# A quarter of the state sum of a scan kernel moved from VectorE to ScalarE and TensorE, with one decay bank fewer

## The reference, cut to what matters

```python
dt = softplus(xc @ dt_w + dt_b);  A = -exp(A_log)
Bm = xc @ B_w;  Cm = xc @ C_w
def step(h, inp):                       # once per token, h is [batch, 512, 16]
    h = exp(dt_t[..., None] * A) * h + dt_t[..., None] * Bm_t * xc_t[..., None]
    y = einsum('bds,bs->bd', h, Cm_t) + D_skip * xc_t
out = ys @ out_proj_w
```

## Time and profile before

| | us |
|---|---|
| median of 3 executions | 1931.46 (1931.4 to 1935.31) |
| the profiled execution | 1939.45 |
| its span in the trace | 1937.8 |
| phase 1, scans of the eight chunks | 80 to 1134.6 of the span |
| a chunk between two starts of scans | 133.5 to 136.4 (the first 118.0, the last 127.6) |
| phase 2 | from about 1200 |
| VectorE busy in the span | 1256.9 |
| GpSimd, ScalarE | 1016.0, 778.9 |
| TensorE, products | 1524.1 |

### The profile page before, as it was taken

One profiled execution on the slowest core, in us unless ns is written; L12 is line 12 of the kernel. 1 busy time (PEld: TensorE's weight loads), 2 busy tenths in 40 slices (PEclk: granted clock), 3 DMA queues, 4 the chain that ended last, 5 costly groups with the idle time before them and its releaser, 6 DMA issues. The chain is left out here.

```text
span 1937.8 us, 22792 instructions
## 1 busy us (share of the span) xinstructions
PE 1524.1 (79%) x6572; PEld 996.6 (51%) x6572; DVE 1256.9 (65%) x2109; ACT 778.9 (40%) x1378; POOL 1016.0 (52%) x1238
## 2 busy tenths in 40 slices
PE   5787888888887888878876665699999999999600
PEld 2344545545544445445445443467777777777400
DVE  1399999999999999998999962112222222222266
ACT  3555456466465566474563432112211222212122
POOL 0669678788688698687787744011111111111274
PEclk9898899999999999999997597799999999999855
DMA  3111121121122012111111101661101111111165
GB/s 90 50 33 47 42 55 47 58 60 52 53 56 71 27 61 76 39 55 60 46 48 60 49 33 62 222 229 34 33 31 33 32 33 33 33 33 33 41 194 174
DMA packets 78326, 122.22 MB, mean 63 GB/s; under 512 B 12256, under 2 KB 47936, under 8 KB 78208
## 3 DMA queue, kind: packets, MB, share of 16 engines
q1 hardware_dynamic: 60640, 80.12, 13.5%
q0 software_dynamic: 13344, 36.46, 5.9%
q10 hardware_dynamic: 4224, 4.19, 0.6%
HBM read 89.15 MB, written 31.59 MB: 62 GB/s over the span
## 5 line engine op out<-in xcount | busy, mean ns | idle before, releaser
L856 POOL TENSOR_TENSOR bb<-u,br 128x512 f32<-128x512 f32 x512 | 647.6, 1273 | 204.5 <-DVE hh L707 202.9
L591 ACT ACTIVATE bA<-dt,a_neg 128x512 f32<-128x512 f32 x512 | 351.5, 690 | 448.3 <-DVE hh L707 447.6
L466 PE MATMUL bH<-ident,hh 128*128 128x128 f32 x2048 | 344.1, 296 | 166.6 <-DVE hh L707 116.5
L466 PEld LDWEIGHTS bH<-ident,hh 128*128 128x128 f32 x2048 | 259.5, 151 | 412.3 <-DVE hh L707 180.0
L724 DVE SCALAR_TENSOR_TENSOR yT<-bH,bc,yT 128x512 f32<-128x512 f32 x480 | 348.4, 726 | 17.6 <-PE bH L466 17.0
L707 DVE TENSOR_TENSOR_SCAN hh<-bA,hl,bb 128x512 f32<-128x512 f32 x256 | 325.4, 1271 | 1.1 <-ACT bA L591 1.1
L707 DVE TENSOR_TENSOR_SCAN hh<-bA,bb 128x512 f32<-128x512 f32 x256 | 309.2, 1209 | 25.0 <-ACT bA L591 15.9
L1249 POOL DMA_DIRECT2D expert_out_scratch<-yt x71 | 38.7, 544 | 481.7 <-DVE yt L1331 472.5
L1120 PE MATMUL bD<-w_d,hT 128*128 x852 | 197.6, 382 | 0.8 <-ACT hT L1291 0.8
L1285 ACT ACTIVATE sgm<-bG 128x352 f32<-128x352 f32 x142 | 58.1, 461 | 325.6 <-PE bG L1077 325.6
L1077 PE MATMUL bG<-w_g,xtT 128*128 x568 | 181.9, 463 | 1.9 <-DMA w_d<-in_L_ffn_Wd_dram 1.3
(11 more groups left out here) (185 smaller groups left out, 1861.2 us busy)
## 6 DMA issues: line engine op xcount, KB each, us to landing
br<-b_scratch SPq DMA_DIRECT2D x128, 256.0 KB, 3.2
xt<-expert_in_scratch POOLq DMA_DIRECT2D x71, 128.0 KB, 2.3
expert_out_scratch<-yt POOLq DMA_DIRECT2D x71, 128.0 KB, 2.0
w_g<-in_L_ffn_Wg_dram SPq DMA_DIRECT2D x8, 704.0 KB, 4.3
w_u<-in_L_ffn_Wu_dram SPq DMA_DIRECT2D x8, 704.0 KB, 5.9
w_d<-in_L_ffn_Wd_dram SPq DMA_DIRECT2D x8, 640.0 KB, 7.0
xp<-in_L_attn_x_dram SPq DMA_DIRECT2D x8, 512.0 KB, 5.0
xr<-in_L_attn_x_dram SPq DMA_DIRECT2D x8, 512.0 KB, 5.0
```

Source lines behind the costliest of these rows:

```text
L466: i = e.transpose(bH[g % NH][:, q * P:(q + 1) * P], hh[:, (n - 1) % 2, q, d * P:(d + 1) * P], ident[:])
L591: e.activation(bA[g % NA][:], dt[c % 2][:, d, :], ACT.Exp, scale=a_neg[:, d, n:n + 1]).then_inc(s_a, 1)
L856: e.tensor_tensor(bb[:, k % NB, :], u[c % 2][:, d, :], br[:, n % NR, :], ALU.mult).then_inc(s_bb, 1)
```

## The change

Row tile d = 0 of each state leaves VectorE. ScalarE multiplies the transposed tile by its column of C into `hs` (two buffers; `act_sum`), and TensorE adds `hs` by a product with the identity into a bank of its own, `bY`, over the 16 states (`pe_add`, in the slot of d = 2). After the last state ScalarE copies `bY` to `yT` (`act_summed`, slot 3 of the next loop). The bank comes from the decays: `NA` is 2, and with it `AHEAD_ACT` is 1. `summed` replaces the waits on a sum, by the semaphore of the engine that does it.

```diff
-NA, NH, NQ = 3, 2, 3
+NA, NH, NQ = 2, 2, 3
...
+        hs = sb("hs", [P, 2, CH])
...
+        bY = bank("bY")
...
+        def summed(e, m):
+            if m % J:
+                e.wait_ge(s_y, (J - 1) * (m // J) + m % J)
+            else:
+                e.wait_ge(s_hs, m // J + 1)
...
             if g >= ND + NH:
-                e.wait_ge(s_y, g - ND - NH + 1)
+                summed(e, g - ND - NH)
...
+        def pe_add(e, c, k):
+            n, d = divmod(k, ND)
+            q = c * NS + n - 1
+            if d != 2 or q < 0:
+                return
+            e.wait_ge(s_hs, q + 1)
+            if q % NS == 0 and q:
+                e.wait_ge(s_y0, q // NS)
+            e.matmul(bY[:], ident[:], hs[:, q % 2, :], start=(q % NS == 0), stop=(q % NS == NS - 1)).then_inc(s_ya, 1)
...
+        def act_sum(e, c, k):
+            n, d = divmod(k, ND)
+            q = c * NS + n - 1
+            if d or q < 0:
+                return
+            e.wait_ge(s_ht, J * q + 1)
+            if q >= 2:
+                e.wait_ge(s_ya, q - 1)
+            if n == 1:
+                emptied(e, "bc", c)
+            cs = q // NS
+            e.activation(hs[:, q % 2, :], bH[(c * SLOTS + k) % NH][:], ACT.Identity, scale=bc[cs % 2][:, 0, NS + q % NS:NS + q % NS + 1]).then_inc(s_hs, 1)
+
+        def act_summed(e, c, k):
+            if k == 3 and c:
+                e.wait_ge(s_ya, NS * c)
+                e.copy(yT[(c - 1) % 2][:, 0, :], bY[:]).then_inc(s_y0, 1)
...
-            if g < ND:
+            if g < ND or d == 0:
                 return
...
                     if 0 <= loop < NCH:
                         act_main(e, loop, k)
+                    if 0 <= loop < NCH or loop == NCH and k < ND:
+                        act_sum(e, loop, k)
+                        act_summed(e, loop, k)
...
                         pe_main(e, loop, k)
+                        pe_add(e, loop, k)
```

More of the change, by code:

```diff
@@ L215, in phase1 @@
         s_cx = sem("s_cx"); s_nx = sem("s_nx"); s_co = sem("s_co"); s_no = sem("s_no"); s_cl = sem("s_cl"); s_nl = sem("s_nl")
-        s_cr = sem("s_cr"); s_cp = sem("s_cp"); s_te = sem("s_te"); s_on = sem("s_on"); s_rt = sem("s_rt")
+        s_cr = sem("s_cr"); s_cp = sem("s_cp"); s_te = sem("s_te"); s_on = sem("s_on"); s_rt = sem("s_rt"); s_hs = sem("s_hs"); s_ya = sem("s_ya"); s_y0 = sem("s_y0")
         s_m = sem("s_m"); s_e2 = sem("s_e2"); s_pos = sem("s_pos"); s_sc = sem("s_sc"); s_shs = sem("s_shs")
@@ L381, in pe_post @@
                 if k == POST[b]:
-                    e.wait_ge(s_y, SLOTS * (c + 1))
+                    e.wait_ge(s_y, (J - 1) * NS * (c + 1))
+                    e.wait_ge(s_y0, c + 1)
                     room(e, b, c)
@@ L513, in act_proj @@
                 if c >= 2:
-                    e.wait_ge(s_y, SLOTS * (c - 1))
+                    e.wait_ge(s_y, (J - 1) * NS * (c - 1))
                 e.copy(bc[par][:].rearrange("p j s -> p (j s)"), at("bc", c)[:, 0:J * 2 * NS]).then_inc(freesem("bc", c), 1)
@@ L718, in dve_sum @@
             if n == 1:
-                if d == 0:
+                if d == 1:
                     emptied(e, "bc", c)
@@ L722, in dve_sum @@
             else:
-                e.wait_ge(s_y, g - 2 * ND + 1)
+                summed(e, g - 2 * ND)
                 e.scalar_tensor_tensor(out=yy[:, d, :], in0=bH[g % NH][:], scalar=cm, in1=yy[:, d, :],
```

## The result

Over six executions each, the changed kernel takes 1914.69 us (1908.72 to 1921.6) and the kernel before 1933.54 (1931.4 to 1936.81): ratio 0.9896, 95% interval 0.9875 to 0.9916, so about 20 us less (18.9 between the medians). The forecast was 24.6 us less and 1907; the time lies in its range, and the direction is the forecast's.

The account below looks back on a forecast made before the run. VectorE, almost without a gap, was taken to bound the eight state space chunks. 82.6 us removed less 7.9, 11.2, 16.8, 7.7, 6.0 and 8.4 of losses left 24.6 us: median 1907, range 1882 to 1936.

Parts of the forecast that it names:

- What it removes: One of four sums on VectorE, 128 in all, each counting its 0.645 us step: 82.6 us off, the ceiling.
- The scaled copy on ScalarE: 128 scaled copies taken at 0.65 us a step, lying under VectorE's scan in an ordinary slot.
- The silu block at slot 13: ScalarE's table loads and silu make slot 15's decay late: 17.2 us over seven chunks, 11.2 net of what returns.
- Slot 32: Four normalisations behind the new sum stall slot 34 by 0.35 us, the late copy adds 0.8: 7.7 us lost.
- Slot 45: The same normalisation block makes slot 47's decay late, 1.0 us in each of six chunks: 6.0 us lost.
- Slots 56 to 63: ScalarE's block at slots 58, 59 makes slot 61's decay late: 2.4 us on average, chunks 1 to 7, 16.8.
- GpSimd: Even chunks' slots 0 and 4 gain nothing, slots 43 to 57 lose 1.0 us, chunk 0 1.5: 8.4 us.
- TensorE: 128 new products, 110 us of work, mostly hidden; excess at slots 0 to 6, 16 to 19, 24 to 31: 7.9 us.
- Rival 1: ScalarE's stalls idle TensorE and its clock drops, 1.3 us more a block: 34 us, 1941, slower; chance 0.17.
- Rival 2: TensorE bounds slots 0 to 20, costing 24 us more: 1931, about no change; chance 0.08.
- Rival 3: Larger gain: only the two silu blocks count, 46.6 us gained, 1885; chance 0.10.
- the real price: With two decay banks, each decay serves a scan one slot earlier, so ScalarE's blocks at slots 13, 32, 45, 58-59 stall VectorE.

Follow-up runs that it names:

- e1: Kernel before with two decay banks in place of three and nothing else; 1945.94 us, ratio 1.0092 to the kernel before.
- e3: Changed kernel without the identity product on TensorE, with two decay banks; 1912.78 us, ratio 0.9924 to the kernel before.
- e5: Changed kernel with ScalarE's four normalisations of slot 32 moved to slot 33; 1904.65 us, ratio 0.987 to the kernel before.
- e2: Changed kernel without the identity product on TensorE, with three decay banks; 1894.5 us, ratio 0.9832 to the kernel before.
- e10: Changed kernel with the moves of e5, e6 and e7 together and slot 45's four normalisations split over 45 and 46; 1892.5 us, ratio 0.982.
- e6: Changed kernel with GpSimd's last product `u` moved from slot 57 to 58, behind the mask `mm_`; 1899.74 us, ratio 0.9856.
- e7: Changed kernel with GpSimd's scatters three slots apart, at slots 2, 5, 8, 11, not two; 1907.73 us, ratio 0.9887.
- e8: Changed kernel with the shared expert's two last projections moved from slots 3 and 5 to 7 and 8, their copies later; 1921.92 us, ratio 0.9948.
- e9: Changed kernel with a third decay buffer, placed in SBUF and not in PSUM; 1990.7 us, ratio 1.0329 to the kernel before.

## Why the prediction was right, and where it was not

**What it removes: right.** The sum's step of 0.645 us counts in full. Rows without a block or a collision fall by 0.66, and slots 24 to 31 and 36 to 43 now take 6.41 to 6.93 us a row in chunks 1 to 7, against 6.45 to 6.9 foretold.

**The scaled copy on ScalarE: right.** 686 ns against the 690 of the decay it was sized by. The estimate from the Trainium skill's figures (ScalarE: Activation LUTs, What ACT_TABLE_LOAD costs) was 706, 3% more than the row shows.

**The silu block at slot 13: mechanism right, net too large.** The scan of slot 15 waits 2.41 us, and slots 12 to 15 lose 2.5 us in odd chunks against 2.45 foretold. The step that failed is what comes back. I took 1.0 us of it in each of six chunks and set 1.0 of TensorE's excess against it in three; slots 16 to 19 in truth came out 0.9 to 2.3 us shorter in chunks 1 to 6, beyond the sum removed. e1 alone gives back 0.5 to 2.3 there, with the sum of slot 16 still on VectorE: the sum waited 2.22 us before, and now VectorE arrives late enough for TensorE to have caught up. A stall in front of another stall costs only the difference: slots 12 to 19 cost 6.0, not 14.2.

**Slot 32: mechanism right, size wrong.** 17.9 us over slots 32 to 43 instead of 7.7. The stall is 0.35 us as foretold; the knock-on was put at 0.8 and is 0.99 and 0.48 on two sums, in a row where TensorE also has the new product, which alone costs 0.81 there in an odd chunk by e3. The 0.99 of slot 34 is still there in e3 and goes with e5, so it is the late copy's; the 0.48 of slot 35 goes in e3. The bank has no part in the size: e2 and e3, with three banks and two, take the same time over slots 32 to 35 in chunks 1 to 6. The forecast had this product at nothing for slots 32 to 43, by comparing four slots' sums of work, and that comparison fails where the work is not spread over the four slots. By its own mark (sums waiting over 35 us in all; 37.9 measured) the step on TensorE was wrong, and it was wrong here.

**Slot 45: right in size, in half of the chunks for another reason.** 5.8 us against 6.0. In odd chunks scan 47 waits 0.80 us for its decay, and a third bank (e2 against e3) gives 0.9 back, the split of e10 0.7. In even chunks it waits 0.57, and neither gives anything back: the wait goes, but the next scan, that of slot 48, then waits longer for `hl`. Chunk 2, after, and then e10:

```profile
423.69 1.22 DVE L746 TENSOR_TENSOR_SCAN hh<-bA,bb 128x512 f32<-128x512 f32 x1 [0.34 <-POOL hl L907]
```

```profile
419.05 1.22 DVE L746 TENSOR_TENSOR_SCAN hh<-bA,bb 128x512 f32<-128x512 f32 x1 [1.01 <-POOL hl L907]
```

There GpSimd takes the gain, and the forecast had its term for GpSimd at other slots.

**Slots 56 to 63: right in size, partly by luck.** 17.5 against 16.8. In chunk 3 scans 60 and 61 wait 2.11 and 0.64, together 2.75, near the 2.8 that the forecast named. In chunks 1, 4 and 5 scan 60 waits only 0.39 to 0.67, and the sum of slot 59 waits 2.0 to 2.4 for transposes ahead of it; over slots 56 to 59 chunks 1, 3 and 5 lose the same 2.9. And 0.8 to 0.9 us a chunk is GpSimd's product ahead of `mm_` (e6), which I had not looked for. e1, the banks alone, has 11.9 of the 17.5.

**GpSimd: right in kind, in part.** Slots 0 to 7 of chunks 2, 4 and 6 gain little: together they change by -0.3 to +0.3 us, not by the -1.3 of two sums. But scan (2,0), still released by `hl`, waits 0.32 to 1.44 us there and no longer 2.33; sums of slots 1, 5 and 7 now wait up to 1.71, 1.09 and 0.46 for transposes ahead of it, and e7 got back little. Slots 48 to 55 lose 1.3 us in each even chunk and 0.3 in odd ones, 6.1 in all, twice the 3.0 foretold; no run divides that further. Where GpSimd costs more than forecast is behind the stalls of slots 32 and 45 in even chunks.

**TensorE: wrong in sum and in place.** 7.9 us were foretold for the product, and by e3 it costs 0.8: 9.0 us at slots 20 to 43, where the forecast had 2.1, and nearly as much given back elsewhere, which it had not at all.

**The rivals.** Rival 1, ScalarE's stalls idle TensorE and its clock drops: refuted. The mean granted clock rose from 0.917 to 0.935, and without the product (e3) it is 0.918, so the product does this, the forecast's own argument against the rival. Rival 2, TensorE bounds slots 0 to 20: slots 0 to 19 lose 11.8 us, not 24 more than the 20.9 foretold; e8 shows what it would have looked like. Rival 3, the larger gain: not so, and e2 says why it can't be had by the bank alone. Perfetto Trace Analysis of the Trainium skill (Identifying Performance Opportunities) says that a gap repeating on the engine that should be saturated can mean too little SBUF or PSUM for the next tile. The gaps at slots 15 and 60 to 61 are that by e1, yet the bank is worth 14.5 us of the 60.3, so this reading covers only a quarter of the loss.

**The two banks are not the real price.** The forecast put 41.7 of its 58.0 us of losses (11.2, 16.8, 7.7 and 6.0) under that title; a third bank gives back 14.3 by e2 and e3, and taking it away costs 14.7 by e1. This is the step of the mechanism that failed, though the time came out in the range. With three banks the same blocks on ScalarE come back as late transposes (49.0 us in e2) and late `hl` (16.7).

**Not settled.** Why e10 gains more in even chunks than its parts do stays open. In e3 the lower clock and the longer wait go together; that the clock came first was not shown. What moves the heads of even chunks between kernels whose edits lie elsewhere is not known either.

## What to carry to other kernels

When an engine without gaps loses work, count each removed step in full, and then price every long block of each in-order queue that feeds it: what a stall costs is the difference to the stall that stood behind it, not its length. Where rare long pieces fall on the same slot as the new work, or ahead of what others wait for, moving them pays: four such moves gave almost as much again (16.8 us of scans) as the change itself (21.6). Whether the same moves would have sped up the kernel before was not run, so their gain can't be put down to the change. Ask also what stands behind the stall that you remove: in even chunks it was GpSimd, and the gain was small or nothing. Look at what stands ahead of a short, much awaited instruction in its queue.

## What was not expected of the hardware

**A scan with both operands in SBUF runs against GpSimd.** With its decay in PSUM no scan of after takes over 1284 ns, whatever GpSimd does; with it in SBUF the mean is 1729 and the longest 4458, yet 1233 where GpSimd is idle at its start, and GpSimd's product goes from 1275 to 1371 ns (e9). A piece of e9, VectorE and then GpSimd:

```profile
403.90 2.70 DVE L746 TENSOR_TENSOR_SCAN hh<-bA,bb 128x512 f32<-128x512 f32 x2
...
408.93 1.87 DVE L746 TENSOR_TENSOR_SCAN hh<-bA,bb 128x512 f32<-128x512 f32 x1
```

```profile
408.44 1.28 POOL L895 TENSOR_TENSOR bb<-u,br 128x512 f32<-128x512 f32 x1 [0.32 <-DVE hh L746]
409.67 1.12 POOL L907 COPY hl<-hh 128x4 f32<-128x4 f32 x1
```

The scan from 408.93 ends at 410.80; at the 1.21 us of its neighbours it would end at 410.14. GpSimd's product lies beside its start until 409.72. The copy `hl` of four columns, 189 ns in after, takes 1.12 us and ends with the scan, at 410.79. SBUF — State Buffer of the Trainium skill (Who interferes with whom) states that a VectorE instruction with two SBUF inputs contends with a GpSimd instruction that reads SBUF, and that the ports they share are an exclusive lock. The trace agrees in kind, and my expectation for e9 had not weighed it. That section has no price for a scan; here, with 170 of 512 scans so placed, phase 1's scans took 78.8 us longer.

**More work made TensorE's clock better.** With 128 products more in phase 1 (some 110 us by the forecast's step) the granted clock from 80 to 1100 went from 0.93 to 0.96; without them and otherwise the same (e3) it is 0.93 again. Two banks alone (e1) have 0.94.
